# Turning the second MLP's normed rows by one transposing DMA per unit

## What is computed

```python
attn_out = attn_out @ out_w + out_b + residual
out = rmsnorm(attn_out, postnorm_w)
out = gelu(out @ mlp_w1 + mlp_b1) @ mlp_w2 + mlp_b2
return out + residual
```

## Time and profile before

| | |
|---|---|
| median of three runs | 1121.99 us |
| span of the profiled execution | 1120.9 us |
| PE busy | 1077.3 us (96%) |
| DVE busy | 973.0 us (87%) |
| ACT busy | 960.3 us (86%) |
| POOL busy | 560.8 us (50%) |
| DMA, mean of the span | 30 GB/s |
| granted clock of TensorE | full, in nearly all of the span |

### The profile page before, as it was taken

How to read it: one execution, slowest core, us unless ns; L and a number is a source line. 1 busy time by engine, 2 the same in 40 slices (tenths; PEclk the granted TensorE clock), 3 DMA queues, 4 the chain that set the end, 5 groups by cost and what they waited for, 6 DMA issues and landing times.

```text
span 1120.9 us, 46846 instructions
## 1 busy us (share of the span) xinstructions
PE 1077.3 (96%) x19624; PEld 942.0 (84%) x19624; DVE 973.0 (87%) x2360; ACT 960.3 (86%) x2155; POOL 560.8 (50%) x807
## 2 busy tenths in 40 slices
PE   6688999999999999999999999999999999999998
PEld 5677788888888888888888888888888888888887
DVE  4899988888899888889988888999888899998774
ACT  3558988998888899988888998888899888899887
POOL 3757555454544545454454445455444555554322
PEclk9999999999999999999999999999999999999999
DMA  7541000000000000000000000000000000000000
GB/s 262 185 163 40 17 19 15 9 15 19 14 13 19 20 15 18 19 14 13 19 19 20 14 18 19 8 19 19 19 15 19 19 8 20 23 8 8 7 7 21
DMA packets 30435, 34.13 MB, mean 30 GB/s; under 512 B 11920, under 2 KB 28048, under 8 KB 29200
## 3 DMA queue, kind: packets, MB, share of 16 engines
q1 hardware_dynamic: 30224, 31.14, 8.7%
HBM read 26.93 MB, written 4.19 MB: 28 GB/s over the span
## 4 chain that ended last, share of the span: by engine, by line
PE 57%; DVE 24%; ACT 7%; POOL 6%; issue 4%; DMA 1%; SPq 0%; DVEq 0%; ACTq 0%; POOLq 0%
PE psum L482 23%; PE psum L662 11%; PE psum L622 6%; PE psum L495 5%; PE psum L456 4%; PE psum L589 3%; PE psum L608 3%; DVE mx_self L1318 3%; POOL prob_self L2561 3%; DVE prob_self L1337 3%; DVE late L1301 3%; DVE prob_self L1308 2%; DVE spread_lat L1268 2%; DVE mx_ctx L1318 2%; ACT xn_mlp L1967 1%
## 5 line engine op out<-in xcount | busy, mean ns | idle before, releaser
L2561 POOL TENSOR_TENSOR prob_self<-prob_self,add_self 128x512 f32<-128x512 f32 x64 | 84.8, 1342 | 146.8 <-DVE prob_self L1308 146.7
L2561 POOL TENSOR_TENSOR prob_cross<-prob_cross,add_cross 128x512 f32<-128x512 f32 x64 | 81.0, 1286 | 88.8 <-DVE prob_cross L1308 88.8
L2040 ACT ACTIVATE staging<-psum,cols,undo_in 128x128 f32<-128x128 f32 x256 | 95.8, 456 | 2.2 <-PE psum L482 1.7
L2040 ACT ACTIVATE hid_mlp<-psum,folded,undo_in 128x128 f32<-128x128 f32 x256 | 97.0, 472 | 0.1
L662 PE MATMUL psum<-hi_m,parts_mlp 128*128 128x256 f16 x512 | 94.6, 273 | 0.9 <-DVE parts_mlp L1370 0.9
L662 PE MATMUL psum<-hi_n,staging 128*128 128x256 f16 x512 | 94.1, 273 | 1.1 <-ACT headsT_lat L1988 0.6
L482 PE MATMUL psum<-xT_mlp,hi_m 128*128 128x128 f16 x1024 | 92.6, 219 | 0.1
L482 PE MATMUL psum<-xT_mlp,hi_n 128*128 128x128 f16 x1024 | 92.5, 219 | 0.0
L2567 POOL TENSOR_TENSOR late<-late,mx_ctx 128x512 f32<-128x512 f32 x64 | 67.2, 1050 | 45.2 <-DVE mx_ctx L1324 42.1
L482 PE MATMUL psum<-xT_mlp,lo_n 128*128 128x128 f16 x512 | 89.0, 219 | 0.0
L482 PE MATMUL psum<-xT_mlp,lo_m 128*128 128x128 f16 x512 | 89.0, 219 | 0.0
(11 more groups left out here) (281 smaller groups left out, 4045.8 us busy)
## 6 DMA issues: line engine op xcount, KB each, us to landing
xin<-in_x SPq DMA_DIRECT2D x32, 128.0 KB, 2.1
ctxT<-in_ctxT SPq DMA_DIRECT2D x32, 128.0 KB, 2.0
late<-in_ctxT SPq DMA_DIRECT2D x4, 1024.0 KB, 9.0
late<-in_x SPq DMA_DIRECT2D x4, 1024.0 KB, 6.6
out<-xb SPq DMA_DIRECT2D x32, 128.0 KB, 2.1
staging<-in_w_m SPq DMA_DIRECT2D x2, 1024.0 KB, 6.6
staging<-in_w_n SPq DMA_DIRECT2D x2, 1024.0 KB, 5.4
mask<-in_mask_cross SPq DMA_DIRECT2D x32, 32.0 KB, 1.9
```

The costliest lines, as they stand in the source:

```text
L2040: last = e.activation(hid[t][g][:, j * P:(j + 1) * P], ps[:, j * P:(j + 1) * P], ACT.Gelu_apprx_tanh, bias=b1[:, 4 * g + j:4 * g + j + 1], ...
L2561: e.tensor_tensor(ch, ch, over_heads(a[:, :]), ALU.add).then_inc(sem["added_" + t], 1)
```

## The change

For `mlp1` alone, the rows are split before they are turned. `high_pair` on ScalarE writes the rows times `rstd` as float16 into `pair[:, 0, :]`. `low_pair` on VectorE takes the product again and subtracts that, into `pair[:, 1, :]`, at the places where `low_half` stood. `turn_across` on SyncE moves the pair, 128 rows of 512 float16 values, by one transposing DMA into `xT_mlp1`; it waits for `low_pair` of the unit, for both `hidden` of the unit before, and for the DMA before. `hidden` of mlp1 waits for that DMA. `turn(u, "mlp1")`, `high_half(u, "mlp1")` and the tile `xn_mlp1` go. `high_pair` stands where `normalize(u, "mlp1")` stood and waits for the DMA before; `root` waits for `low_pair` of the unit before. In SyncE's list `turn_across(t - 6)` comes last in the slot; in the epilogue it is placed between stores. In the diff `across_mlp1` is the DMA's semaphore.

```diff
             def hidden(u, t, g, b):
                 q.wait_ge("lo_mlp", {"mlp0": 1, "mlp1": 4}[t])
-                q.wait_ge("x_lo_" + t, u + 1)
+                if t == "mlp1":
+                    q.wait_ge("across_mlp1", 16 * (u + 1))
+                else:
+                    q.wait_ge("x_lo_" + t, u + 1)
...
                 score(t - 2, "self", 2)
-                turn(t - 6, "mlp1", 5)
                 v_cross(t - 3, 4)
...
+            @of_unit
+            def low_pair(u):
+                q.wait_ge("x_hi_mlp1", u + 1)
+                e.scalar_tensor_tensor(pair[:, 1, :], residual("mlp1", u)[:, :], rstd["mlp1"][:, 0:1], pair[:, 0, :],
+                                       ALU.mult, ALU.subtract).then_inc(sem["x_lo_mlp1"], 1)
...
+            @of_unit
+            def high_pair(u):
+
+                q.wait_ge("across_mlp1", 16 * u)
+                q.wait_ge("rstd_mlp1", u + 1)
+                e.activation(pair[:, 0, :], residual("mlp1", u)[:, :], ACT.Copy, scale=rstd["mlp1"][:, 0:1]).then_inc(sem["x_hi_mlp1"], 1)
...
-                normalize(t - 6, "mlp1")
+                high_pair(t - 6)
...
-                high_half(t - 6, "mlp1")
...
-                q.wait_ge("xn_" + t, u)
+                q.wait_ge("x_lo_mlp1" if t == "mlp1" else "xn_" + t, u)
...
+            def turn_across(u):
+
+                q.wait_ge("x_lo_mlp1", u + 1)
+                q.wait_ge("hid_mm_mlp1", 2 * u)
+                q.wait_ge("across_mlp1", 16 * u)
+                e.dma_start_transpose(xT["mlp1"][:, :, :].bitcast(F16).rearrange("p k t -> p (k t)").rearrange("p (j t) -> p j t", j=2 * KH),
+                                      pair[:, :, :].rearrange("p i h -> p (i h)")).then_inc(sem["across_mlp1"], 16)
...
+            turn_across(0)
             for t in range(FILL, SLOTS):
                 load_x(t)
                 load_rest(t)
                 store(t - 10)
+                turn_across(t - 6)
```

More of the change, by code:

```diff
@@ L247, in build @@
         xb = [sb(f"xb{i}", [P, H]) for i in range(IN_FLIGHT)]
-        xn = {t: sb("xn_" + t, [P, H]) for t in ("self", "cross", "mlp0", "mlp1")}
+        xn = {t: sb("xn_" + t, [P, H]) for t in ("self", "cross", "mlp0")}
+        pair = sb("pair_mlp1", [P, 2, H], F16)
         heads = {t: sb("heads_" + t, [P, H]) for t in ("self", "cross", "lat")}
-        xT = {t: sb("xT_" + t, [P, KH, P]) for t in ("self", "cross", "mlp0", "mlp1")}
+        NORMED = ("self", "cross", "mlp0", "mlp1")
+        xT = {t: sb("xT_" + t, [P, KH, P]) for t in NORMED}
         headsT = {t: sb("headsT_" + t, [P, KH, P]) for t in ("self", "cross", "lat")}
@@ L1605, in _ @@
             largest_score(2, "lat", 0)
-            low_half(0, "mlp1")
+            low_pair(0)
             largest_score(2, "lat", 1)
@@ L1649, in _ @@
                 divided(t - 5, "lat")
-                low_half(t - 6, "mlp1")
+                low_pair(t - 6)
                 largest_score(t - 2, "self", 0)
@@ L1720, in _ @@
             masked(UNITS - 4, "ctx", 0)
-            low_half(UNITS - 6, "mlp1")
+            low_pair(UNITS - 6)
             masked(UNITS - 4, "ctx", 1)
@@ L1770, in _ @@
             lat_low(UNITS - 3)
-            low_half(UNITS - 5, "mlp1")
+            low_pair(UNITS - 5)
             denominators(UNITS - 2, "cross")
@@ L1827, in _ @@
             k_spread(UNITS - 2, "lat", 1)
-            low_half(UNITS - 4, "mlp1")
+            low_pair(UNITS - 4)
             add_residual(UNITS - 1, "cross")
@@ L1850, in _ @@
             q_bias_lat(UNITS - 1)
-            low_half(UNITS - 3, "mlp1")
+            low_pair(UNITS - 3)
             k_spread(UNITS - 1, "lat", 0)
@@ L1873, in _ @@
             divided(UNITS - 1, "lat")
-            low_half(UNITS - 2, "mlp1")
+            low_pair(UNITS - 2)
             add_residual(UNITS - 1, "lat")
@@ L1877, in _ @@
             hidden_lo(UNITS - 3, "mlp1", 1)
-            low_half(UNITS - 1, "mlp1")
+            low_pair(UNITS - 1)
             hidden_lo(UNITS - 2, "mlp1", 0)
@@ L2179, in _ @@
             prob_out(1, "lat", 1)
-            normalize(0, "mlp1")
+            high_pair(0)
             heads_out(1, "lat")
-            high_half(0, "mlp1")
             normalize(3, "mlp0")
@@ L2244, in _ @@
             gelu(UNITS - 7, "mlp1", 1)
-            normalize(UNITS - 6, "mlp1")
+            high_pair(UNITS - 6)
             prob_out(UNITS - 5, "lat", 1)
@@ L2290, in _ @@
             exponential(UNITS - 2, "cross", 1)
-            normalize(UNITS - 5, "mlp1")
+            high_pair(UNITS - 5)
             prob_out(UNITS - 2, "cross", 0)
@@ L2328, in _ @@
             exponential(UNITS - 1, "cross", 1)
-            normalize(UNITS - 4, "mlp1")
+            high_pair(UNITS - 4)
             lat_out(UNITS - 2)
@@ L2350, in _ @@
             prob_out(UNITS - 2, "ctx", 1)
-            normalize(UNITS - 3, "mlp1")
+            high_pair(UNITS - 3)
             prob_out(UNITS - 2, "lat", 1)
@@ L2371, in _ @@
             prob_out(UNITS - 1, "lat", 1)
-            normalize(UNITS - 2, "mlp1")
+            high_pair(UNITS - 2)
             hidden_hi(UNITS - 3, "mlp1", 0)
@@ L2375, in _ @@
             heads_out(UNITS - 1, "lat")
-            high_half(UNITS - 2, "mlp1")
             hidden_hi(UNITS - 3, "mlp1", 1)
             gelu(UNITS - 2, "mlp1", 0)
-            normalize(UNITS - 1, "mlp1")
+            high_pair(UNITS - 1)
             hidden_hi(UNITS - 2, "mlp1", 0)
-            high_half(UNITS - 1, "mlp1")
             gelu(UNITS - 2, "mlp1", 1)
@@ L2860, in _ @@
             store(UNITS - 8)
+            turn_across(UNITS - 6)
             store(UNITS - 7)
+            turn_across(UNITS - 5)
             store(UNITS - 6)
+            turn_across(UNITS - 4)
             store(UNITS - 5)
+            turn_across(UNITS - 3)
             store(UNITS - 4)
+            turn_across(UNITS - 2)
+            turn_across(UNITS - 1)
             store(UNITS - 3)
```

38 lines of the change are left out of this document (12 added, 26 removed).

## The result

The changed kernel takes 1127.24 us (median of four runs, 1126.46 to 1128.13) against 1122.22 us for the kernel before in the same session: a ratio of 1.0045, 95% interval 1.0031 to 1.0059. It is slower, inside the range, but by 5.0 us and not by 12.9. The profiled execution spans 1124.6 us; that of before spans 1120.9.

The account below looks back on a forecast made before the run. A chain of waits bounds each slot, about 21 us on TensorE, then 11.6 on VectorE and neighbours. Port block 4.3 + DMA waits 2.2 + 1.55 + 5.2 - 0.3 = 12.9 us on 1122.0: 1134.9 us, range 1124 to 1147.

Parts of the forecast that it names:

- L: Time from SyncE's release of the transposing DMA to its landing, taken as 4.1 us, between 2.1 and 8.4.
- the three terms of the ends: TensorE's uncovered waits for the DMA: 2.2 us at unit 0, 1.55 at unit 29, 5.2 at units 30 and 31.
- the 0.17 us of the port block: In each of 25 slots, GpSimd's mask addition delays low_pair and so VectorE's maximum by 0.17 us: 4.3 us.
- What bounds a slot: Main loop: about 21 us of each slot bound by TensorE, 11.6 us by VectorE and its neighbours; period 32.6 us.
- goes on without a gap: In each slot VectorE was said to run unbroken from the maximum at 607.54 to the norm of mlp0.
- my sign of being wrong: Period staying at 32.6 us though low_pair is stretched would mean slack in the slot's chain.
- The two products, 0 us: Removing mlp1's turn from TensorE saves nothing in the 25 slots, its 0.27 us each covered by prob_turn's wait.
- The copies, 0 us: Removing high_half and putting high_pair for normalize on ScalarE costs or saves 0 us, being off the slot's chain.
- my estimate of 5.2 us: Alternative DMA latency from the skill's 1309 ns per 128x128 block, four blocks, giving 1139.3 us in all.
- Where the consumer waits: hidden of mlp1: DMA covered up to 9.5 us in slots; waits at units 0, 29, 30 and 31.
- The forecast case: Both costs, port block in the slots and DMA waits at the ends: 12.9 us, chance 0.62.
- nothing shows: Rival: no port block in the slots and DMA latency near 2.1 us, 1123.1 us, within 0.2%; chance 0.09.

Follow-up runs that it names:

- e12: Kernel before, but low_half of mlp1 in the 25 slots subtracts from the normed rows in SBUF, not the PSUM bank: 1124.16 us.
- e3: Changed kernel, but low_pair reads a PSUM bank in the 25 slots and a spare ScalarE copy takes high_half's place: 1127.33 us.
- e2: Changed kernel plus one unread ScalarE copy in each of the 25 slots, in high_half's place: 1127.41 us.
- e4: Kernel before without high_half of mlp1 in the 25 slots: 1121.12 us, ratio 1.0001.
- e1: Changed kernel, but low_pair in the 25 slots reads a PSUM bank in place of the residual rows: 1128.33 us.
- e11: Changed kernel with two tiles for the turned rows and two for the pairs, used in turn: 1127.71 us.
- e7: Changed kernel with two transposing DMAs per unit, the first into a tile nobody reads; hidden waits for both: 1140.73 us.
- e9: Changed kernel with two transposing DMAs per unit and unread matmuls on TensorE during its DMA waits at units 0, 29, 30 and 31: 1133.87 us.

## Why the prediction was right and wrong, step by step

The mechanism was the forecast one, and two terms of the sum were mis-sized. L was put at 4.1 us and measured 2.5 to 3.0 from the pair to its first product, which took the three terms of the ends from 8.95 to 3.5 us. And the 0.17 us of the port block were put on the chain in full, 4.3 us, where 0.075 us a slot, 1.9 us, reached it, because VectorE was waiting there for the mix already.

- *What bounds a slot.* Right that the chain leaves TensorE at the scores of `self`, and that 779 of 782 us busy don't make TensorE the bound: 6.7 us less work there made nothing faster. Wrong in "goes on without a gap": there was a second path, 0.09 us later than VectorE's. It shows in no idle record, only in the steps between starts (0.68 against 0.59 us). The period, 32.69 us for a forecast of 32.8, says the same: my sign of being wrong, slack where I saw none, came half true.
- *The two products, 0 us.* Right in the changed kernel (e12 has them and the same slot, to 0.003 us). The wait of `prob_turn` took the saving as said (0.40 us in the changed kernel's slot, 0.21 before), but `v_cross` and its copy did come 0.26 us earlier and the mix 0.15. Without the block that is worth something (e3: 0.067 us a slot).
- *The copies, 0 us.* Right in the changed kernel (e2: +0.002 us a slot); 0.025 to 0.033 us a slot without the block (e4, and e3 against e1).
- *low_pair.* Its record (0.79 us, 0.47 alone) and the 0.17 us on the maximum were right. The mis-sized term is what reaches the slot: 0.075 us, so 1.9 us in 25 slots for 4.3. Missed: 2.4 us. e12 shows the same with nothing else changed.
- *L, the DMA.* Mis-sized, the largest part. 4.1 us taken; 2.4 from issue to landing in the median, and 2.8, 2.4, 2.6 and 2.4 at units 0, 29, 30 and 31. From the end of low_pair to TensorE's first product it is 2.5 at unit 29 (1087.62 to 1090.12), 2.7 at unit 30 (1103.83 to 1106.56) and 3.0 at unit 0 (157.9 to 160.89). I had let each of four blocks be issued as a small load is; SyncE issues the whole in 1.2 us (1.6 at unit 0). Of the two pages of the Trainium skill, Advanced Engine Details and Errata, "X-Bar Transpose (TRN2)", was the nearer: 2.4 us against 2.1 for a plain load of this size. The 1309 ns of the Trainium skill, VectorE: DVE Perf Modes, "The three transpose paths", are for one 16-bit block; my estimate of 5.2 us from them, four blocks one after the other, is not borne out, and no run here moves one block alone.
- *Where the consumer waits*. Right: slots covered, waits at units 0, 29, 30 and 31, the one of unit 29 small. The reason given for unit 31, one tile only, was not what bound: with two tiles the end is 0.1 to 0.2 us shorter (e11), and the same dependence on unit 30 came over ScalarE's order. With L = 3.0 at unit 0, 2.5 at unit 29 and 2.7 after, the recorded terms give 1.1, 0, 2.4 and -0.3, in sum 3.2 us; measured in the profiled executions 1.2 + 2.0 = 3.2. With L of 4.1 they were 8.65. Missed: 5.4 us, and with the 2.4 above that is the whole error of 7.9.
- *What had no term:* the clock behind an idle TensorE. It cost nothing in the changed kernel's profiled execution, 6.9 us in e7, and is over a third of the cost once L is about what I thought (3.8 to 5.4 us in e7, 19.0 us over before).
- *The order of chances.* The forecast case (block and uncovered ends) is what happened, each at less than its price. The rival "nothing shows", which needed no block and an L near 2.1, had the size of L nearly right. The 1127.4 us that the prediction works out for L = 2.1 is all but the measured time, by luck: its L is too short and its block too dear, and the two errors cancel.

## What to carry to other kernels

Before a stretch of an engine is called gapless, compare the steps between the starts of its instructions with the same steps elsewhere: a wait of 0.09 us is marked nowhere, and it halves what a delay of 0.17 us costs. An off-engine path with a latency belongs where it has cover; keep the old way at the first and last units, where it has none (2.3 against 5.0 us over before, here). And price an idle time of TensorE at more than its length.

## What the runs showed of the hardware

- A `scalar_tensor_tensor` (changed kernel) or `tensor_tensor` (e12) of VectorE with two SBUF tensors, beside a GpSimd addition, ends 0.28 us after that addition's recorded end, in every slot: it takes 0.79 us, where the first takes 0.47 alone. The addition that GpSimd starts next then takes 1.46 us in place of 1.27. With one of VectorE's inputs in PSUM neither is delayed (0.47 us in e1, 0.41 in the kernel before).
- A transposing DMA of 128 rows of 512 float16 values, SBUF to SBUF, lands 2.4 us after its issue in the median and up to 4.1 in the changed kernel (4.6 in e3), and keeps SyncE 1.2 us (2.1 at most). A second one behind it on the queue comes 1.25 us later (e7). The whole kernel's DMA packets rose from 30435 to 47843; the plain loads of 128 KB landed after 2.2 us, before after 2.1.
- Where TensorE had stood idle for 2.9 us (e7, to 165.88) its granted clock was 0.50 from 165 to 170 and 0.85 from 170 to 175. With 1.3 us idle in the changed kernel it was 1.00, and so with 1.38 in e11, but with 1.39 in e1 0.71, and with 2.6 in e3 1.00. Matmuls on data that nobody reads, run during the wait, kept it full (e9).
